# The image part of the experts' second product, four rows together in 32-column groups

## The reference, cut to what matters

```python
B, T, H, F, E = (128, 32, 192, 768, 3)      # here: 32 rows, 153 tokens
scores = jax.nn.softmax(jnp.mean(x, axis=1) @ Wg.T, axis=-1)
_, idx = jax.lax.top_k(scores, 1)
sel = idx[:, 0]
h = jax.nn.gelu(jnp.einsum('bth,ehf->betf', x, W1) + b1[None, :, None, :], approximate=False)
y = jnp.einsum('betf,efh->beth', h, W2) + b2[None, :, None, :]
w = scores * jax.nn.one_hot(sel, E, dtype=scores.dtype)
out = jnp.einsum('beth,be->bth', y, w)
```

## Time and profile before

| | |
|---|---|
| median of three executions | 1160.63 us |
| the profiled execution | 1158.21 us, span 1156.4 us, mean granted TensorE clock 0.809 |
| whole span: TensorE / VectorE / ScalarE busy | 65% / 84% / 65% |
| expert stage | from about 986 us to the end |
| DMA over the span | 54.57 MB, mean 47 GB/s |

### The profile page before, as it was taken

One profiled execution on the slowest core, in us unless ns is written; L12 is line 12 of the kernel. 1 busy time (PEld: TensorE's weight loads), 2 busy tenths in 40 slices (PEclk: granted clock), 3 DMA queues, 4 the chain that ended last, 5 costly groups with the idle time before them and its releaser, 6 DMA issues. The chain is left out here.

```text
span 1156.4 us, 23186 instructions
## 1 busy us (share of the span) xinstructions
PE 745.9 (65%) x6175; PEld 527.2 (46%) x6176; DVE 970.8 (84%) x2490; ACT 752.8 (65%) x1304; POOL 152.6 (13%) x265
## 2 busy tenths in 40 slices
PE   4761156574888566666666666666652398699997
PEld 3640044342555333333333433333321286699986
DVE  5777889788888799999999999999999881467666
ACT  0351000594888889999999999999983175355553
POOL 5840000004665000000000000000000630000000
PEclk9985567897999777788788788778755677799999
DMA  5001000000111111000000000110003000455542
GB/s 161 3 2 68 0 0 0 1 0 18 36 37 37 35 27 22 21 21 21 21 21 21 21 21 21 24 22 20 18 6 143 12 1 1 171 188 178 197 169 101
DMA packets 84367, 54.57 MB, mean 47 GB/s; under 512 B 53832, under 2 KB 83304, under 8 KB 84072
## 3 DMA queue, kind: packets, MB, share of 16 engines
q1 hardware_dynamic: 83304, 53.97, 15.3%
q0 software_dynamic: 1024, 0.13, 0.2%
HBM read 11.77 MB, written 3.76 MB: 13 GB/s over the span
## 5 line engine op out<-in xcount | busy, mean ns | idle before, releaser
L1240 DVE SCALAR_TENSOR_TENSOR expo<-expo,con,pow 128x153 f32<-128x153 f32 x480 | 146.1, 375 | 0.7 <-ACT expo L1174 0.7
L1069 PE MATMUL at_pT<-identb,vi 128*128 128x128 bf16 x480 | 62.3, 297 | 88.7 <-ACT vi L1148 88.0
L613 ACT ACTIVATE qi<-pq,biasp,ap 128x306 int16<-128x306 f32 x96 | 47.9, 722 | 94.0 <-PE pq L571 94.0
L1053 PE MATMUL at_rem<-below,identb 128*128 128x459 bf16 x160 | 68.1, 426 | 61.8 <-ACT expo L1174 60.8
L1174 ACT ACTIVATE expo<-at_rem,con 128x459 f32<-128x459 f32 x160 | 96.7, 641 | 15.7 <-PE at_rem L1054 7.9
L882 DVE TENSOR_REDUCE rs_ends<-rs_banks 128x770 f32 (+1 forms) x96 | 91.5, 959 | 14.0 <-PE rs_banks L853 11.9
L802 ACT ACTIVATE rs_banks<-rs_banks 128x770 f32<-128x770 f32 x96 | 76.3, 798 | 25.0 <-PE rs_banks L845 24.4
L1137 ACT ACTIVATE octave<-at_banks,con 128x459 int16<-128x459 f32 x160 | 90.2, 650 | 1.2 <-PE at_banks L708 0.2
L703 PE MATMUL at_banks<-pick,row_top 128*128 128x459 bf16 x160 | 78.1, 488 | 19.6 <-ACT octave L1137 18.0
L1069 PEld LDWEIGHTS at_pT<-identb,vi 128*128 128x128 bf16 x480 | 43.6, 132 | 103.3 <-issue 76.4
L1289 DVE CUSTOM_DVE_ANT_0 weight_top<-weight_top,line 128x2448 uint16<-128x2448 uint16 x64 | 83.8, 1350 | 8.1 <-ACT line L1165 5.8
(11 more groups left out here) (380 smaller groups left out, 2171.5 us busy)
## 6 DMA issues: line engine op xcount, KB each, us to landing
qk<-vt SPq DMA_DIRECT2D x64, 384.0 KB, 3.1
rs_kb<-qk SPq DMA_DIRECT2D x128, 28.7 KB, 1.9
kb<-qk SPq DMA_DIRECT2D x128, 28.7 KB, 2.0
patches<-in_patches SPq DMA_DIRECT2D x4, 768.0 KB, 10.1
vi<-vt SPq DMA_DIRECT2D x32, 96.0 KB, 2.0
out<-vi SPq DMA_DIRECT2D x32, 96.0 KB, 1.7
pj_w<-in_w SPq DMA_DIRECT2D x1, 2304.0 KB, 8.4
qb<-qk SPq DMA_DIRECT2D x128, 6.0 KB, 1.8
```

The costliest lines, as they stand in the source:

```text
L1053: pe.matmul(out, identb[:, :], bank(below, b), start=True, stop=False)
L1069: mm = pe.transpose(pT[:, slot, j * P:(j + 1) * P], src, identb[:, :])
L1240: ins = v.scalar_tensor_tensor(ex[:, t, :], ex[:, t, :], c(7), pw[:, t, :].bitcast(BF16), ALU.add, ALU.mult, accum_out=tot[:, t:t + 1])
```

## The change

The image part of the second product leaves the single row and is done for a group of four rows at once. For each of the four, the stationary operand is 32 tokens wide (`gi`, high and low parts apart), and the result goes to its own 32 partitions of `p3`, that is to its own column group of the array; 18 x 4 = 72 matmuls per group. The moving operand no longer is addressed in `w2h` and `w2l` by the expert's number: SyncE reads `sel` a second time (`image_weights`) and copies the row's two `w2` parts (128 x 2304 B each) into one of four slots of a fixed buffer `w2s`. VectorE casts text and image parts apart in `split`; `collect` loses its two image additions; `image` reads four expert numbers, adds the bias to each row's 32 partitions and scales as before. The image steps stand one step later than before (at kk = 1 and 5 of eight), and the written-out body has 8 steps.

```diff
-    RING = SLOTS = 4
-    HI, BOTH, LO = slice(0, NT), slice(IW, IW + 64), slice(N + 32, N + 32 + NT)
+    RING, SLOTS = 8, 4
+    HI, LO = slice(0, NT), slice(NT, 2 * NT)
...
-        gs = sb("e_gs", [P, 2, FT, N + 32 + NT], BF16)
+        gs, gi = sb("e_gs", [P, 2, FT, 2 * NT], BF16), sb("e_gi", [P, RING, FT, 2, 32], BF16)
+        w2s = m["qkflat"][:, 12288 + 4 * FT * N:12288 + 4 * FT * N + SLOTS * 2 * FT * C].rearrange("p (s i f c) -> p s i f c", s=SLOTS, i=2, f=FT)
...
+        def group(c, kk):
+            if kk % 4 != 1 or isinstance(c, int) and not 1 < c * RING + kk <= B + 1:
+                return None
+            return c * 2 + kk // 4 - 1, (kk // 4 - 1) % 2
...   (SyncE)
+                def image_weights(n, slot, grp):
+                    e = sp.value_load(sel[0:1, ds(n, 1)], min_val=0, max_val=E - 1)
+                    if not (isinstance(n, int) and n < SLOTS):
+                        wait_apart(sp, i_acc, grp, k.passed)
+                    for i, w in enumerate((w2h, w2l)):
+                        sp.dma_start(w2s[:, slot % SLOTS, i, :, :], w[:, e, :, :]).then_inc(w2_in, 16)
                 def body(c, kk):
-                    now, gone = batch(c, kk, 0), batch(c, kk, 4)
+                    now, gone, mid = batch(c, kk, 0), batch(c, kk, 4), batch(c, kk, 3)
                     if now is not None:
-                        weights(now[0], now[1])
+                        weights(now[0], now[1] % SLOTS)
                     if gone is not None:
-                        rows(*gone)
+                        rows(gone[0], gone[1] % 4, gone[2])
+                    if mid is not None:
+                        image_weights(*mid)
                 steps(sp, body)
-                for n in range(B - 3, B):
+                image_weights(B - 1, B - 1, G - 1)
+                for n in range(B - 2, B):
                     rows(n, n % 4, n // 4)
...   (TensorE)
-                    wait_apart(pe, i_bias, n + 1, k.passed)
-                    parts = [(w, f) for f in range(FT) for w in (w2h, w2l)]
-                    for b, (w, f) in enumerate(parts):
-                        mm = pe.matmul(p3[0:64, u, 0:C], gs[:, u, f, BOTH], w[:, e, f, :], start=(b == 0), stop=(b == 2 * FT - 1))
                     mm.then_inc(y_acc, 1)
+                def image_product(grp, w):
+                    wait_apart(pe, i_bias, grp * 4 + 4, k.passed)
+                    pe.wait_ge(w2_in, grp * 128 + 128)
+                    parts = [(a, x, f) for f in range(FT) for a, x in ((0, 0), (0, 1), (1, 0))]
+                    for b, (a, x, f) in enumerate(parts):
+                        for j in range(4):
+                            mm = pe.matmul(p3[32 * j:32 * j + 32, w, 0:C], gi[:, 4 * w + j, f, a, :], w2s[:, j, x, f, :],
+                                           start=(b == 0), stop=(b == 3 * FT - 1))
+                    mm.then_inc(i_acc, 1)
                 def body(c, kk):
...
                     if last is not None:
                         second_product(last[0], last[1], e_last)
+                    if img is not None:
+                        image_product(*img)
...   (VectorE)
-                    v.tensor_copy(gs[:, u, :, 0:N], g[:, u, :, :]).then_inc(g_hi, 1)
-                    v.wait_ge(g_hi, n + 1)
+                    if not (isinstance(c, int) and c == 0):
+                        v.wait_ge(i_acc, c * 2 + slot // 4 - 1)
+                    v.tensor_copy(gs[:, u, :, HI], g[:, u, :, 0:NT]).then_inc(g_hi, 1)
+                    v.tensor_copy(gi[:, slot, :, 0, :], g[:, u, :, IW:N]).then_inc(g_hi, 1)
+                    v.wait_ge(g_hi, n * 2 + 2)
                     v.tensor_tensor(gs[:, u, :, LO], g[:, u, :, 0:NT], gs[:, u, :, HI], ALU.subtract).then_inc(g_split, 1)
-                    v.tensor_tensor(gs[:, u, :, N:N + 32], g[:, u, :, IW:N], gs[:, u, :, IW:N], ALU.subtract).then_inc(g_split, 1)
+                    v.tensor_tensor(gi[:, slot, :, 1, :], g[:, u, :, IW:N], gi[:, slot, :, 0, :], ALU.subtract).then_inc(g_split, 1)
...
                     v.tensor_tensor(yb[:, u, :], p2[:, u, 0:C], b2[:, e, :], ALU.add).then_inc(y_bias, 1)
-                    v.wait_ge(i_out, grp + 1)
-                    v.tensor_tensor(yi[r, :], p3[0:32, u, 0:C], b2[0:32, e, :], ALU.add).then_inc(i_half, 1)
...
-                    v.wait_ge(i_half, n + 1)
-                    v.tensor_tensor(yi[r, :], p3[32:64, u, 0:C], yi[r, :], ALU.add).then_inc(i_bias, 1)
-                def image(grp):
-                    v.wait_ge(i_bias, grp * 4 + 6)
+                def image(grp, w):
+                    es = [expert(grp * 4 + j) for j in range(4)]
+                    v.wait_ge(i_acc, grp + 1)
+                    v.wait_ge(i_out, grp + 1)
+                    for j in range(4):
+                        r = slice(32 * j, 32 * j + 32)
+                        v.tensor_tensor(yi[r, :], p3[r, w, 0:C], b2[r, es[j], :], ALU.add).then_inc(i_bias, 1)
+                    v.wait_ge(i_bias, grp * 4 + 12)
                     v.wait_ge(image_sent, grp * 64 + 64)
                     v.scalar_tensor_tensor(oi[:, :], yi[:, :], gwi[:, ds(grp, 1)], Hres[:, B + grp, :], ALU.mult, ALU.add).then_inc(i_out, 1)
```

More of the change, by code:

```diff
@@ L1709, in experts @@
         p1, p2, p3 = k.ps("e_p1", [P, 2, 2, 512], F32, st), k.ps("e_p2", [P, 2, 512], F32, st), k.ps("e_p3", [P, 2, 512], F32, st)
-        h_acc, h_act, g_hi, g_split, g_room, y_acc, y_bias, y_out, i_half, i_bias, i_out = (
-            k.sem("e_" + x) for x in ("h_acc", "h_act", "g_hi", "g_split", "g_room", "y_acc", "y_bias", "y_out", "i_half", "i_bias", "i_out"))
+        h_acc, h_act, g_hi, g_split, g_room, y_acc, y_bias, y_out, i_acc, i_bias, i_out = (
+            k.sem("e_" + x) for x in ("h_acc", "h_act", "g_hi", "g_split", "g_room", "y_acc", "y_bias", "y_out", "i_acc", "i_bias", "i_out"))
         w_in = [k.sem(f"e_w_in{j}") for j in range(SLOTS)]
+        w2_in = k.sem("e_w2_in")
         sent = [k.sem(f"e_sent{j}") for j in range(4)]
@@ L1722, in steps @@
                     body(i, kk)
-            body(B // RING, 0)
+            for kk in range(2):
+                body(B // RING, kk)
         def batch(c, kk, lag):
@@ L1729, in batch @@
                 return None
-            return c * RING + kk, kk % RING, c + kk // RING
+            return c * RING + kk, kk % RING, c * 2 + kk // 4
+        def group(c, kk):
+            if kk % 4 != 1 or isinstance(c, int) and not 1 < c * RING + kk <= B + 1:
+                return None
+            return c * 2 + kk // 4 - 1, (kk // 4 - 1) % 2
         with k.nc.Block() as block:
@@ L1766, in _, with first_product @@
                 expert = lambda n: pe.value_load(sel[0:1, ds(n, 1)], min_val=0, max_val=E - 1)
-                def first_product(n, kk):
-                    u = kk % 2
+                def first_product(n, slot):
+                    u, kk = slot % 2, slot % SLOTS
                     pe.wait_ge(h_act, n * FT + FT)
@@ L1789, in second_product @@
                         mm = pe.matmul(p2[:, u, 0:C], gs[:, u, f, a], w[:, e, f, :], start=(b == 0), stop=(b == 3 * FT - 1))
-                    wait_apart(pe, i_bias, n + 1, k.passed)
-                    parts = [(w, f) for f in range(FT) for w in (w2h, w2l)]
-                    for b, (w, f) in enumerate(parts):
-                        mm = pe.matmul(p3[0:64, u, 0:C], gs[:, u, f, BOTH], w[:, e, f, :], start=(b == 0), stop=(b == 2 * FT - 1))
                     mm.then_inc(y_acc, 1)
+                def image_product(grp, w):
[7 more added lines that the diff above has]
+                    mm.then_inc(i_acc, 1)
                 def body(c, kk):
-                    now, last = batch(c, kk, 0), batch(c, kk, 1)
+                    now, last, img = batch(c, kk, 0), batch(c, kk, 1), group(c, kk)
                     e_last = expert(last[0]) if last is not None else None
@@ L1823, in _ @@
                 v.sem_inc(y_bias, 2)
-                v.sem_inc(i_bias, 2)
+                v.sem_inc(i_bias, 8)
                 v.sem_inc(y_out, 1)
@@ L1845, in split, with collect @@
                         v.wait_ge(y_acc, n - 1)
-                    v.tensor_copy(gs[:, u, :, 0:N], g[:, u, :, :]).then_inc(g_hi, 1)
-                    v.wait_ge(g_hi, n + 1)
+                    if not (isinstance(c, int) and c == 0):
[3 more added lines that the diff above has]
+                    v.wait_ge(g_hi, n * 2 + 2)
                     v.tensor_tensor(gs[:, u, :, LO], g[:, u, :, 0:NT], gs[:, u, :, HI], ALU.subtract).then_inc(g_split, 1)
-                    v.tensor_tensor(gs[:, u, :, N:N + 32], g[:, u, :, IW:N], gs[:, u, :, IW:N], ALU.subtract).then_inc(g_split, 1)
+                    v.tensor_tensor(gi[:, slot, :, 1, :], g[:, u, :, IW:N], gi[:, slot, :, 0, :], ALU.subtract).then_inc(g_split, 1)
                     v.wait_ge(g_split, n * 2 + 2)
                     v.sem_inc(g_room, 1)
-                def collect(n, j, grp):
-                    u, r = j % 2, slice(32 * j, 32 * j + 32)
```

(11 more changed lines are left out.)

## The result

The changed kernel takes 1241.21 us (median of four, 1240.35 to 1241.59) against 1161.22 for the kernel before (1156.34 to 1164.04): ratio 1.069, 95% interval 1.066 to 1.073. It is slower by 80 us. The forecast was 1222 with a range of 1190 to 1250. The profiled execution of the changed kernel has a span of 1239.3 us.

The account below looks back on a forecast made before the run. The prediction took TensorE to set the pace before and SyncE's queue after the change: +53 over six groups, +4 at the start, +1 in the last group and 5 for the clock, +63 on 1158, say 1222 us; range 1190 to 1250.

Parts of the forecast that it names:

- SyncE's queue is the bound: Expert stage, third rival and the forecast itself: SyncE's list of reads and issues limits, 1222 us; chance 0.84.
- ledger: SyncE's work per four rows: 16.4 us plus 9.2 for four added calls, 25.6 us, above every other engine.
- One call: One image_weights on SyncE, a read, check, wait and two copies: 1.8 to 2.5 us, taken as 2.3.
- exposure: SyncE's wait at i_out: 6.5 us from last image copy issue, less 3.75 of other work, 2.75 exposed per four rows.
- The clock term: TensorE's image product after idling: a low clock would add 1.5 us each time; half taken, 5 us over seven groups.
- The column groups: TensorE's 72 image matmuls in 18 sets of four column groups overlap: 1.7 us per four rows, 6.2 if not.
- The fourth rival: TensorE's image product: the four column groups' loads do not hide, 36 us more, 1258 us; chance 0.05.
- The sum: Whole stage: +53 over six groups, +4 at the start, +1 in the last group, 5 for the clock, +63 us.
- The traffic: DMA: 3.6 MB per four rows plus 2.4 MB more, 213 GB/s, counted as hidden.
- The first rival: Expert stage: prefetch hides SyncE's work, TensorE stays the bound, 25 us less, 1133 us; chance 0.05.
- the opening: Kernel before, expert stage: TensorE sets the pace, busy 19.85 and 19.81 of 20 us, 4.71 us a row.
- The second rival: Expert stage: SyncE keeps up, VectorE becomes the bound at 20.2 to 21 us, +5 to +11, 1166; chance 0.06.

Follow-up runs that it names:

- e4: Kernel before, with SyncE's added reads and two copies per row in its list, nothing reading the copies: 1211.1 us, ratio 1.041.
- e3: Changed kernel, with SyncE's wait at i_out and the four image output copies moved one step later: 1212.5 us, ratio 1.043 to the kernel before.
- e7: e3 without VectorE's reads and additions in the image step, bias added beforehand by GpSimd: 1214.3 us.
- e1: Changed kernel, SyncE copying image weights for the first four rows only, all groups using these copies: 1203.5 us, 1.035.
- e2: Changed kernel, with the image weight reads and copies issued by GpSimd in place of SyncE: 1211.6 us, 1.044.
- e5: Changed kernel with both edits, image copies issued by GpSimd and image outputs one step later on SyncE: 1200.3 us, 1.033.
- e9: Changed kernel, image weights copied for the first four rows only, image outputs one step later, bias added beforehand by GpSimd: 1172.7 us, 1.011.
- e12: Complete computation: changed kernel, image copies on GpSimd, image outputs one step later, bias folded in beforehand, ScalarE's loop written out: 1165.3 us, 1.006.
- e11: e9 with ScalarE's loop over pairs of rows written out, one table load left of 16: 1154.5 us, 0.998 against the kernel before.
- e10: Kernel before with 2 of the 12 image matmuls per row, the other ten left out: 1162.0 us against 1159.1, ratio 1.000.
- e6: e5 without VectorE's image-step reads and bias additions, GpSimd adding the weighted bias to the residual rows beforehand: 1176.1 us, 1.011.
- e8: Kernel before with only SyncE's second read of the expert's number, its check and a wait per row, no copies: 1164.8 us against 1158.7, 1.005.

## Why the prediction was right, and where it was not

*The bound named.* "SyncE's queue is the bound" held: e4 adds only its work and loses 50 us; e3 and e7 stand at its 26 us a pass. Its ledger was 16.4 + 9.2 = 25.6 us; measured 26.3. One call was put at 2.3 and is 2.4, by the rows without waits (6.14 less 3.75 us). Its two issues take 1.23 us from the first one's start to the second one's end, where 0.9 to 1.0 was reckoned, since they are 0.56 and 0.54 and not 0.36 to 0.43; the rest of the call came out 0.2 shorter than reckoned.

*The exposure and the clock.* 4.3 us were exposed a pass, 2.75 expected, and half of 1.5 us for the clock on top. From the start of the last issue to the outputs it is 1126.04 - 1117.72 = 8.3 us where the sum had 6.5; the image product is 1.4 of the difference (3.07 and not 1.7), VectorE 0.5 (2.2 with the hand-over inside it, 1.74 reckoned). SyncE's own work meanwhile is 4.0 (3.75). Without the clock's 1.4 the exposure is 2.9, nearly as reckoned. The clock term is what was mis-sized: the full 1.4 came in six of the eight groups, and two were free of it. The product took 1.67 us in the first and the third group, where TensorE had been idle 1.5 and 2.4 us ahead of it, and 3.01 to 3.07 us in the others, idle 4.8 to 5.7 us ahead. In e1, e2 and e5, without such a gap, the product takes 1.67 us in the first seven groups. TensorE's other matmuls run in part at the low clock too; they are not the limit, but they are why its busy share is 0.68 to 0.70 and not the 0.55 that the prediction gave as a sign.

*The column groups.* 1.7 us at the full clock was exact. The fourth rival is out:

```profile
L1825 PEld LDWEIGHTS e_p<-qk,e_gi x576: 92/97/150, 1025.3 to 1164.7; 128*32 128x32 bf16 x192
L1825 PE MATMUL e_p<-qk,e_gi x576: 246/246/368, 1025.3 to 1164.8; 128*32 128x192 bf16 x192
```

These are e9's: 72 loads of 97 ns in 1.67 us must overlap. The statement of the Trainium skill ("TensorE: Matmul & The Clock Gate", section "Part 3: Packing small matmuls — row/col tiling"), that a load overlaps with matmuls in flight only where the row group differs, does not hold for these column groups. The same section's table of packed products gives 2.38 times for three column groups, which agrees in kind.

*The sum.* By the two profiled executions 83 us were added. 6 lie ahead of the change, as said above, and 77 in the stage, where the forecast had 63. The 20 us that 1158 + 63 falls short of the profiled 1241 are so 14 in the stage and 6 from outside it. In the stage, from the first group's image outputs to the seventh's, six passes added 67 us and not 53 + 5 = 58: passes of 30.6 and not 28.4 + 0.7. From SyncE's first read to the first image outputs 6 were added and not 4. The last pass took 20.2 us, as reckoned (20), but the prediction set it against a pass of 19.6 where the kernel before has 15.9 at this place: 4 were added and not 1.

*The traffic.* Costed at nothing, it cost nothing while SyncE issued it (share 0.54 as before, 2.6 us to land). Once the passes shorten to 18 to 20 us, the copies cost something: e12 takes 11 us more than e11.

*The first rival and the opening.* Here the prediction was wrong without harm to its number. "So TensorE sets the pace" rested on 99% busy and on the chain of waits, and from it came 25 us of gain for the case that SyncE keeps up. e10 takes those 3.3 us away and gains nothing. TensorE, VectorE (put at 18.3, own need 18.9) and the chain within a row stand at nearly one height. e9 takes all added costs outside TensorE away and is still 1.1% slower than the kernel before (1.006 to 1.015); e11, with ScalarE's loop written out too, is level with it. Had SyncE had room, the change would have brought nothing or a small loss, not -25.

*The second rival* had VectorE's own list at 20.2 to 21 us. With SyncE relieved by leaving the copies out (e1), a pass less VectorE's waits for gelu is 21.2 us, so the list was right there. What else is in e1's 25.6, the circle and the waits for gelu, the rival did not have. With GpSimd's copies (e5) the list is 23.5: the idle time ahead of the image step grows from 2.7 to 4.9 to 5.2 us. The loss is then still 42 us and not 5 to 11. How much of that is VectorE's list and how much the chain through gelu was not separated beyond e6 and e11.

## What to carry to other kernels

An engine that only issues copies has no busy share; count its list (reads, waits, issues) over one pass before giving it more, because here its slack was 3.2 us and the change asked for 9.8. Replacing an address from a register by a copy into a fixed buffer only moves the register work, and adds issues. When the engine at 99% is relieved, first try the relief alone with part of its work left out: that run (e10) would have told that there was nothing to win.

## What the runs showed of the hardware

A copy of 128 x 2304 B took SyncE 0.432 us to issue from DRAM and 0.52 to 0.58 from SBUF to SBUF (64 issues of the changed kernel). The read of one number from SBUF into a register on SyncE depends on what stands before it: in e8 the reads of `weights`, mostly 1.0 us or more behind the last issue, have a median of 0.27 us, those of the added `image_weights`, 0.14 us behind an output copy, of 0.80. VectorE's reads in the changed kernel range from 0.30 to 0.90 too, though it issues no copies; what lengthens them was not tested. Beside copies issued by GpSimd, SyncE's reads have a median of 0.88 us (e6) where they have 0.54 without them (e9), and its image outputs take up to 1.27 us to issue and not 0.43; between e1 and e2, with passes over 25 us, the same comparison shows no such growth (0.87 and 0.86). A loop around gelu on ScalarE brings an ACT_TABLE_LOAD of 1.28 us in each turn, 16 in all; written out, one is left. TensorE's product in four column groups (72 matmuls of 32 columns) takes 1.67 us at the full clock and 3.07 at half of it.
